# Graph layer kernel: all gather indices kept in SBUF, GpSimd copies each half visit's columns, SyncE loads no indices and issues the query rows first

## The reference

```python
x_norm = _layernorm(x, ln_g, ln_b)
q = x_norm @ Wq.T + bq
k = x_norm @ Wk.T + bk
v = x_norm @ Wv.T + bv
dk = silu(edge_attr @ Wdk.T + bdk)
dv = silu(edge_attr @ Wdv.T + bdv)
q_i, k_j, v_j = q[dst], k[src], v[src]
attn = jnp.sum(q_i * k_j * dk, axis=1)
attn = silu(attn) * _cosine_cutoff(edge_weight)
msg = v_j * dv * attn[:, None]
agg = segment_sum(msg, dst, num_segments=x.shape[0])
return x + agg @ Wo.T + bo
```

## Time and profile before

| what | us |
|---|---|
| median of 3 runs | 2869.73 (2869.44 to 2889.89) |
| span of the profiled execution, first to last instruction | 3160.5 |
| before the first visit | 319.9 |
| first to last `e_place`, 97 visits | 2733.1 |
| from the last `e_place` to the end | 107.5 |

### The profile page before, as it was taken

How to read it: one execution, slowest core, us unless ns; L and a number is a source line. 1 busy time by engine, 2 the same in 40 slices (tenths; PEclk the granted TensorE clock), 3 DMA queues, 4 the chain that set the end, 5 groups by cost and what they waited for, 6 DMA issues and landing times. The chain is left out here.

```text
span 3160.5 us, 51763 instructions
## 1 busy us (share of the span) xinstructions
PE 2407.8 (76%) x12012; PEld 1957.1 (62%) x12012; DVE 2155.2 (68%) x6159; ACT 1916.8 (61%) x4051; POOL 2135.0 (68%) x1792
## 2 busy tenths in 40 slices
PE   6388777787877877878777887878868778787787
PEld 5144666665666656666666665666656566665666
DVE  4366767676676766767677776766767667676676
ACT  2265566665666656656566665656656556565665
POOL 1656767677666776667766777777767767777672
PEclk9599889889888988889889998898989989899898
DMA  7676766767677676767776767767776766767664
GB/s 221 147 186 244 203 196 200 213 189 215 194 210 207 201 211 192 210 204 206 216 203 200 227 198 212 202 198 213 204 209 200 217 197 201 213 195 215 201 197 165
DMA packets 321332, 642.50 MB, mean 203 GB/s; under 512 B 83932, under 2 KB 141648, under 8 KB 321304
## 3 DMA queue, kind: packets, MB, share of 16 engines
q0 software_dynamic: 129840, 418.60, 46.3%
q1 hardware_dynamic: 191464, 223.60, 23.6%
HBM read 583.26 MB, written 58.74 MB: 203 GB/s over the span
## 5 line engine op out<-in xcount | busy, mean ns | idle before, releaser
L949 POOL DMA_INDIRECT e_kv<-kv_tab,e_idx x1568 | 1957.1, 1248 | 802.0 <-issue 681.8
L1081 ACT ACTIVATE e_gate<-e_gate_ps 128x1024 f32<-128x1024 f32 x786 | 806.2, 1026 | 616.4 <-remote 364.5
L1153 DVE TENSOR_TENSOR e_gated<-e_kv,e_gate 128x1024 f32<-128x1024 f32 x788 | 960.6, 1219 | 292.2 <-ACT e_gate L1081 149.2
L1000 PE MATMUL e_sum_ps<-e_gated,weighed_hot 128*128 128x256 f32 x3168 | 895.5, 408 | 98.7 <-ACT weighed_hot L1097 75.3
L1012 PE MATMUL e_gate_ps<-wd_hi_lo,high 128*128 128x512 f32 x1572 | 769.0, 489 | 35.5 <-ACT e_gate L1081 21.9
L1163 DVE CUSTOM_DVE_ANT_0 e_gated<-e_gated,e_q_ps 128x256 f32<-128x256 f32 x1576 | 591.2, 409 | 282.1 <-remote 232.7
L1031 PE MATMUL e_q_ps<-q_win,hot_t 128*128 128x256 f32 x1572 | 456.8, 316 | 406.9 <-issue 301.2
L1000 PEld LDWEIGHTS e_sum_ps<-e_gated,weighed_hot 128*128 128x128 f32 x3168 | 622.2, 206 | 200.8 <-ACT weighed_hot L1097 82.4
L1013 PE MATMUL e_gate_ps<-wd_bias,low 128*128 128x512 f32 x1572 | 644.8, 410 | 0.0
L1031 PEld LDWEIGHTS e_q_ps<-q_win,hot_t 128*128 128x128 f32 x1572 | 325.0, 207 | 485.0 <-issue 411.2
L1097 ACT ACTIVATE weighed_hot<-hot,e_attn 128x128 f32<-128x128 bf16 x1580 | 515.1, 399 | 26.5 <-issue 13.5
(11 more groups left out here) (156 smaller groups left out, 1459.7 us busy)
## 6 DMA issues: line engine op xcount, KB each, us to landing
e_attr<-attr_groups_dram SPq DMA_DIRECT2D x784, 128.0 KB
e_kv<-kv_tab,e_idx POOLq DMA_INDIRECT x1568
e_q_next<-q_tab SPq DMA_DIRECT2D x98, 256.0 KB
sum_tab<-e_sums SPq DMA_DIRECT2D x100, 128.0 KB
e_prior<-sum_tab SPq DMA_DIRECT2D x99, 128.0 KB
kv_tab<-l_kv_out SPq DMA_DIRECT2D x49, 256.0 KB
q_tab<-l_q_out SPq DMA_DIRECT2D x49, 256.0 KB
sum_tab<-zeros SPq DMA_DIRECT2D x25, 256.0 KB
```

Source lines behind the costliest of these rows:

```text
L949: pool.indirect_dma_start(kv[:, k, :], None, kv_tab, bass.IndirectOffsetOnAxis(ap=idx[:, k:k + 1], axis=0)).then_inc(kv_landed[k // G][k % ...
L1000: last = nc.tensor.matmul(sum_ps[:, 0:H], weighed_hot[:, c % 2, k, :], gated[:, c * G + k, H:2 * H], start=(c == 0 and k == 0), stop=(c == ...
L1081: nc.scalar.activation(gate[:, 2 * p:2 * p + 2, :], gate_ps[:, 2 * p:2 * p + 2, :], ACT.Silu).then_inc(silu_ready[s][p], 1)
L1153: nc.vector.tensor_tensor(gated[:, pair(s, p), :], kv[:, pair(s, p), :], gate[:, 2 * p:2 * p + 2, :], ALU.mult).then_inc(gated_ready[s][p], 1)
```

## The change

A tile `e_idx_all` holds the indices of all blocks (128 x 1568 integers, 6.3 KB in each partition); one DMA on SP fills it before the loop. SP no longer loads indices in the loop, so `idx_free`, its increments and the waits on the other half's landings go. SP's first item in each visit is now the query rows. POOL copies eight columns of `e_idx_all` into `e_idx` ahead of tile 0 and of tile 8, waits for its own copy, and goes on gathering. POOL's loop over all visits becomes a loop over blocks with an inner loop over the block's visits, with one value loaded from SBUF for each block.

```diff
+        idx_all = sb("idx_all", [P, BLOCKS * BLOCK_TILES], I32)
...
-                def load_idx(half, t):
-                    sp.wait_ge(go, 1)
-                    sp.wait_ge(idx_free[half], visit.prev)
-                    sp.dma_start(idx[:, half * HALF:(half + 1) * HALF],
-                                 src_tiles[:, bass.ds(t * BLOCK_TILES + half * HALF, HALF)]).then_inc(idx_landed[half], 16)
...
+                sp.dma_start(idx_all[:], src_tiles).then_inc(idx_landed, 16)
                 with sp.Fori(0, BLOCKS) as t:
                     n = visits(sp, t)
                     node = sp.value_load(walk[0:1, 1, bass.ds(t, 1)], min_val=0, max_val=N - 1)
                     with sp.Fori(0, n) as r:
-                        load_idx(0, t)
-                        load_attr(0, t)
-                        load_attr(1, t)
-                        load_idx(1, t)
-                        load_attr(2, t)
-                        load_attr(3, t)
                         sp.wait_ge(go, 1)
                         sp.wait_ge(q_ready, visit.prev)
                         sp.dma_start(q_next[:], q_tab[bass.ds(window_row(sp, node, r), P), :]).then_inc(q_landed, 16)
+                        load_attr(0, t)
+                        load_attr(1, t)
+                        load_attr(2, t)
+                        load_attr(3, t)
...
-                def gather_half(half):
-                    pool.wait_ge(go, 1)
-                    pool.wait_ge(idx_landed[half], visit.now16)
-                    for k in range(half * HALF, (half + 1) * HALF):
+                def gather_half(half, t):
+                    first = half * HALF
+                    for k in range(first, first + HALF):
                         if k % 2 == 0:
                             nearer = (k - AHEAD) % BLOCK_TILES
                             pool.wait_ge(go, 1)
                             pool.wait_ge(gated_ready[nearer // G][nearer % G // 2], visit.of(k, AHEAD))
                             pool.wait_ge(go, 1)
                             pool.wait_ge(gated_ready[k // G][k % G // 2], visit.prev)
+                        if k == first:
+                            nc.gpsimd.tensor_copy(idx[:, first:first + HALF],
+                                                  idx_all[:, bass.ds(t * BLOCK_TILES + first, HALF)]).then_inc(idx_ready[half], 1)
+                            pool.wait_ge(go, 1)
+                            pool.wait_ge(idx_ready[half], visit.prev2)
                         gather(k)
-                        if k == half * HALF + FREED - 1:
-                            before = 1 - half
-                            for s in (2 * before, 2 * before + 1):
-                                for p in range(2):
-                                    pool.wait_ge(kv_landed[s][p], visit.now32 if half else visit.late32)
-                            pool.sem_inc(idx_free[before], 1)
...
-                with pool.Fori(0, all_visits(pool)):
-                    gather_half(0)
-                    gather_half(1)
-                    visit.step()
+                pool.wait_ge(idx_landed, 16)
+                with pool.Fori(0, BLOCKS) as t:
+                    n = visits(pool, t)
+                    with pool.Fori(0, n):
+                        gather_half(0, t)
+                        gather_half(1, t)
+                        visit.step()
```

More of the change, by code:

```diff
@@ L839, in edge_stage @@
         sum_ps = psum("sum_ps", [P, 2 * H], F32)
-        attr_landed, idx_landed, q_landed = sems("attr_landed", GROUPS), sems("idx_landed", 2), sem("q_landed")
-        q_ready, idx_free = sem("q_ready"), sems("idx_free", 2)
+        attr_landed, idx_landed, q_landed = sems("attr_landed", GROUPS), sem("idx_landed"), sem("q_landed")
+        q_ready, idx_ready = sem("q_ready"), sems("idx_ready", 2)
         kv_landed = [sems(f"kv_landed{i}_", 2) for i in range(GROUPS)]
@@ L940, in _ @@
             def _(pool):
-                visit = Visits(pool, "pool_e", "cur prev now16 now32 late32")
+                visit = Visits(pool, "pool_e", "cur prev prev2")
                 pool.sem_inc(go, 1)
-                pool.sem_inc(idx_free[0], 2)
-                pool.sem_inc(idx_free[1], 1)
-                FREED = 3
                 AHEAD = 10
```

## The result

Slower, by 2.1 per cent. The changed kernel takes 2936.16 us (median of 4 runs, 2911.85 to 2950.53) where the kernel before took 2873.82 beside it: ratio 1.0206, interval 1.0157 to 1.0255. A second comparison gave 2931.86 against 2878.42, ratio 1.0207 (1.0143 to 1.0271). The forecast was 2820; the time lies inside the range given (2690 to 2970), on the side of rival 1.

The account below looks back on a forecast made before the run. POOL was taken as nearly the bound, 24.8 us of a 25.2 us visit. Gathers 20.0, collisions 3.6 and copies 1.3 made 24.9 us a visit, 2440 for 98; with time outside and start, forecast 2820 us, range 2690 to 2970.

Parts of the forecast that it names:

- rival 1: POOL's queue becomes the bound without its breaks: collisions 4.8, copies 1.3, 26.1 us a visit, 2958 us; chance 0.32.
- the sum's collision term: POOL's gathers held up by DVE's gate multiplications: 3.6 us a visit taken, in POOL's need.
- the middle of the first two: Collisions between 4.8 us a visit (gathers fall at random) and 2.4 (about half remains when DVE waits for POOL).
- The copy term: Two POOL copies a visit, each 0.15 us plus 0.8 wait less 0.3 gap: 1.3 us a visit, bounds 0.6 and 1.8.
- The 3 us for the start: 784 KB of indices must land before the first gather: up to 3 us, once.
- POOL's need of 24.8 us: POOL's time a visit before the change: 16 gathers, 20.0 us, plus 4.8 us of collisions; runs at 25.2.
- The removed waits: ACT's 291.9 us for query rows and SP's waits for POOL go; POOL's waits for landings are worth nothing.
- The signs listed: Waits said to show the forecast right, including DVE's wait for gathers growing from 74.6 to over 200 us.
- it was said to tell at 1.25: A mean POOL gather above 1.25 us would show the forecast wrong, by collisions.
- "Remote" stalls: ACT's 364.5 us in 96 waits without a cause in the program, taken as largely the profiled execution's own.
- Rival 2: Long visits are real in the runs too, the profile only stretches everything by a tenth: 2690 us; chance 0.16.

Follow-up runs that it names:

- e1: The kernel before, unchanged, run again for a second profiled execution: 2860.27 us, ratio 0.9967.
- e2: The kernel before with only the query rows issued first in SP's loop, index loads kept: 2876.73 us, ratio 0.9986.
- e13: The kernel before with the gate's silu left in PSUM, so DVE's multiplication reads one operand from SBUF and one from PSUM: 2617.54 us, ratio 0.9117.

## Why the prediction was wrong

**The step that failed is the sum's collision term.** The prediction took 3.6 us a visit, "the middle of the first two", on the argument that a DVE that waits for its gathers shifts them away from its multiplications. Measured: 4.5. DVE did wait for a gather at 359 of 788 multiplications, and 706 of the 788 still held up a gather, nine in ten and not half: with gathers 1.25 us apart when undisturbed and a multiplication of 1.22 us, almost every multiplication meets the start of one. The term did fall, from the 5.1 us of e1 (16 x (1.266 - 0.95)), but by 0.5 and not by 1.2. The 4.8 us of the trace, one of the prediction's two bounds, was much nearer; that half would remain had no row behind it.

**The copy term was mis-sized too.** 1.3 us a visit was taken, 1.66 measured. The stand was 0.75 us (taken: 0.8), but the copy itself is not 0.15 us: it is 0.20 when alone and 0.38 on average, since it collides as well (48 of the 196 copies take over 0.5 us). The 3 us for the start had no row either; the first visit begins at 289.0 us here and at 287.9 in e1. Together the two terms miss by 0.9 + 0.36 = 1.3 us a visit, some 124 us of 98 visits; 2820 and 124 make 2944, and 2936 were measured.

**Rival 1 came, at nearly its price.** It had 4.8 + 1.3 and 2958 us, deciding "from collisions plus copies above 5.2 us"; they were 6.2. Its reason against, that the phase of a POOL-bound loop is another, fell.

**The bound was read nearly right, and its consequence not used.** POOL's need of 24.8 us against a visit of 25.2 already said that nothing beside POOL could gain over 39 us. Shown by e1 and e2: it gained nothing. A change that adds certain work to the engine so close to the bound, and takes nothing off it, needs a falling collision term to win; the whole forecast hung on that.

**The removed waits.** The 291.9 us of ACT went, as predicted, and what was late next was POOL, as predicted. The signs listed came: no wait at the copy of the query rows, SP waiting for DVE and ACT, POOL idle in gaps and behind copies, 512.0 us of DVE for gathers, no alternation. They held whichever way the time went, so they could not tell the forecast from rival 1; only the mean gather could, and it was said to tell at 1.25. It came at 1.233, under that mark, and the kernel was slower. The mark was wrong, since the kernel before itself has 1266 in e1. The span too fell by 215.6 us, as was said, but not for the reason given: in e1 that of the kernel before is 2854.7, so the change raised it by 90, and the rest lies between the chips.

**"Remote" stalls as part of the profiled execution.** Partly wrong. In the experiments they come with one of four chips, and there every execution is long (all seven of the kernel before took 3130 to 3154), so they are most likely the chip's and not the profile's. That the runs to be predicted are without them was right. Rival 2, which had the long visits as real, is half true: e1 has them, up to 31.8 us beside 21, but POOL works through them, and nothing was gained. Its reason against, that instructions have the same length in every visit, holds for DVE (19.45 and 19.94 us busy) but not for PE (19.81 and 23.18, at a granted clock of 1.00 and 0.85).

**The rule of the Trainium skill** (SBUF — State Buffer, Who interferes with whom) did better than the sum. That a GpSimd instruction which reads SBUF is blocked for a VectorE instruction's whole length was seen for a copy: 1.27 us beside a multiplication of 1.23. The reverse was not seen: the multiplication takes 1219 to 1223 ns on average in every kernel with collisions. The same section says that an instruction of VectorE with at most one SBUF input, outside the two-port modes, does not contend; e13 agrees, with a mean gather of 977 ns against 1266.

Left open: the cause of the unnamed stalls and of the fourth chip's results, and what a gather's 0.3 us of gap consists of.

## What to carry to other kernels

When one engine's need is within a few per cent of the loop, price the change on that engine alone: waits that vanish elsewhere move, they don't pay. Ask first what lengthens that engine's instructions; here one operand's place was worth 9 per cent, and only then did the stall of the query rows, worth nothing before, become worth 5. And take a collision term from what the trace shows unless a row says that the phase will change.

## What the runs showed of the hardware

- An indirect DMA on GpSimd, 128 rows of 2 KB, takes 0.95 us with nothing in its way; one that begins inside a VectorE multiplication of two SBUF operands (1.22 us) ends some 0.8 us after it, and so do many that begin up to 0.24 us ahead of it. With one operand in PSUM it is not delayed, and the multiplication is no slower (1213 against 1220 ns).
- A copy of 128 x 8 integers on GpSimd takes 0.20 us; a gather that depends on it begins 0.75 us after its end; one that doesn't, 0.16 us after.
- With pauses on GpSimd the mean gather is lower (1300, 1233, 1173 ns with no, one and two waited copies for each half, query rows first in all three), and where a pause of VectorE goes it is higher (1266 to 1300). Two profiles of the changed kernel gave 1233 and 1224.
- Chips differ: the same program took some 2875 us on three and 3140 on a fourth, and there an edit worth 9 per cent elsewhere made it 2 per cent slower.
